# The tail of a four-layer kernel without six groups of filler matrix products on TensorE

## The reference, cut to what matters

```python
# third layer, feed-forward: a router picks 8 of 64 experts, and each expert is only a bias row
logits = flat @ router_weight.T + router_bias
scores = softmax(logits)
topk_w, topk_idx = top_k(scores, 8)
w_dense = zeros((T, E)).at[arange(T)[:, None], topk_idx].add(topk_w)
out = flat * topk_w.sum(-1, keepdims=True) + w_dense @ expert_bias

# fourth layer, attention: channels split by the top 60% of the context's channels, then gated
mask = one-hot of top_k(channel_map, k)
crucial, sub = mask * x, (1 - mask) * x
A1 = sigmoid(relu(norm(conv1d([max(crucial), mean(crucial)], conv_w))))
A2 = sigmoid(relu(norm(conv1d([max(sub), mean(sub)], conv_w))))
out = crucial * A1 + sub * A2

# fourth layer, feed-forward: a dense product and 2 of 8 low-rank adapters
out = x @ Wb.T + bias + 2 * sum over 2 of 8 adapters e of p_e * (x @ A_e.T) @ B_e.T
```

## Time and profile before

| what | value |
|---|---|
| median of 3 runs | 857.73 us (855.31 to 858.05) |
| the profiled execution | 857.56 us |
| its span | 855.9 us |
| TensorE busy | 774.1 us, 90% |
| VectorE busy | 709.6 us, 83% |
| ScalarE busy | 517.4 us, 60% |
| mean granted TensorE clock, share of full speed | 0.976 |
| start of the tail's work | 777.42 us |

### The profile page before, as it was taken

One profiled execution on the slowest core, in us unless ns is written; L12 is line 12 of the kernel. 1 busy time (PEld: TensorE's weight loads), 2 busy tenths in 40 slices (PEclk: granted clock), 3 DMA queues, 4 the chain that ended last, 5 costly groups with the idle time before them and its releaser, 6 DMA issues. The chain is left out here.

```text
span 855.9 us, 16356 instructions
## 1 busy us (share of the span) xinstructions
PE 774.1 (90%) x5134; PEld 629.4 (74%) x5140; DVE 709.6 (83%) x1752; ACT 517.4 (60%) x1407; POOL 432.1 (50%) x388
## 2 busy tenths in 40 slices
PE   1976799858988999999999999999999999888788
PEld 0474676534677898898898888888888889765347
DVE  7878998969787887887897897897898898786876
ACT  6865798746466657557557657657656565531521
POOL 3237078715036745844845845746646655573110
PEclk9999999979999999999999999999999999999989
DMA  8254236544120310310320320320320210003001
GB/s 313 92 167 155 76 131 223 175 133 144 30 71 22 115 39 9 99 65 0 98 74 0 98 74 0 98 74 0 98 74 0 74 59 15 25 1 120 1 0 50
DMA packets 37773, 66.15 MB, mean 77 GB/s; under 512 B 5537, under 2 KB 17889, under 8 KB 37602
## 3 DMA queue, kind: packets, MB, share of 16 engines
q1 hardware_dynamic: 37730, 65.63, 23.5%
HBM read 60.28 MB, written 5.34 MB: 77 GB/s over the span
## 5 line engine op out<-in xcount | busy, mean ns | idle before, releaser
L2042 ACT ACTIVATE layer_attention_probs<-xnT,stats 128x512 f32<-128x512 f32 x128 | 93.9, 734 | 132.6 <-DVE stats L2177 132.6
L2395 DVE TENSOR_SCALAR_CACHE_REDUCE xn<-ctxT,candidate 128x512 bf16<-128x512 f32 x240 | 168.8, 741 | 0.0
L1781 PE MATMUL bank<-layer_attention_keysT,layer_attention_queriesT 128*128 128x512 f32 x384 | 121.3, 424 | 5.0 <-DVE layer_attention_queriesT L2170 5.0
L2189 DVE TENSOR_TENSOR layer_attention_probsT<-bank,layer_attention_probsT 128x512 fp32r<-128x512 f32 x128 | 88.2, 689 | 41.7 <-ACT layer_attention_probsT L2050 40.3
L1781 PEld LDWEIGHTS bank<-layer_attention_probsT,layer_attention_values 128*128 128x128 f32 x768 | 99.1, 190 | 17.4 <-DVE layer_attention_probsT L2189 6.7
L1781 PE MATMUL bank<-layer_attention_probsT,layer_attention_values 128*128 128x256 f32 x768 | 102.6, 283 | 8.1 <-DVE layer_attention_probsT L2189 6.6
L2050 ACT CAST layer_attention_probsT<-bank 128x512 fp32r<-128x512 f32 x128 | 74.8, 585 | 48.0 <-PE bank L1858 47.9
L1781 PE MATMUL bank<-layer_attention_l_wq,layer_attention_xnT 128*128 128x512 f32 x408 | 99.3, 392 | 0.0
L1781 PEld LDWEIGHTS bank<-layer_attention_l_wkv,layer_context_parts 128*128 128x128 f32 x720 | 88.4, 188 | 2.7
L1781 PE MATMUL bank<-layer_attention_l_wkv,layer_context_parts 128*128 128x256 f32 x720 | 90.4, 278 | 0.0
L1781 PE MATMUL bank<-layer_attention_wo,layer_attention_headsT 128*128 128x512 f32 x336 | 88.8, 406 | 0.0
(11 more groups left out here) (337 smaller groups left out, 1664.7 us busy)
## 6 DMA issues: line engine op xcount, KB each, us to landing
layer_attention_l_raw_qo<-in_wqT SPq DMA_DIRECT2D x8, 1024.0 KB, 5.5
layer_attention_l_raw_qo<-in_woT SPq DMA_DIRECT2D x8, 1024.0 KB, 6.4
xnT<-inverse_sums SPq DMA_DIRECT2D x15, 512.0 KB, 3.7
tw_raw<-in_w_gateT SPq DMA_DIRECT2D x8, 688.0 KB, 5.4
tw_raw<-in_w_upT SPq DMA_DIRECT2D x8, 688.0 KB, 4.3
tw_raw<-in_w_downT SPq DMA_DIRECT2D x6, 768.0 KB, 4.7
layer_attention_l_raw_kv<-in_wkvT SPq DMA_DIRECT2D x8, 512.0 KB, 4.9
ternary<-tw_rounded SPq DMA_DIRECT2D x8, 344.0 KB, 2.6
```

Of the source, the lines that this page charges most:

```text
L1781: last = pe.matmul(out, stationary[f][a], moving[f][b], start=f == 0 and x == 0, stop=f == count - 1 and x == 2)
L2042: a.activation(probs[:, u % 3, :], masked[:, u % 2, :], ACT.Exp, bias=negmax[:, u:u + 1], scale=-1.0, accum_out=sums[:, u:u + 1]).then_inc ...
L2189: v.tensor_tensor(probsT[:, 1, p % 2, :, columns], T[u % 2][:, :].rearrange("p (c q) -> p c q", c=CPB), probsT[:, 0, p % 2, :, columns], A ...
L2395: own(k.nc.vector.tensor_scalar((k.flags if flags is None else flags)[:, r % 2], row_tile(k.ctxT, r), k.candidate[:, r:r + 1].bitcast(F32) ...
```

## The change

The six calls of `keep_busy` and the helper itself are taken out. All other instructions on all engines are the same and in the same order; only line numbers behind the helper are lower by 5 to 11.

```diff
--- before.py
+++ after.py
@@ -2549,11 +2549,6 @@
 
             @block.tensor
             def _(pe):
-                def keep_busy(bank, count):
-                    for _ in range(count):
-                        pe.matmul(k.bank[bank][:, :], k.ident16[:, :],
-                                  k.ident16[:, :].unsqueeze(1).broadcast_to([P, KT, P]), start=True, stop=True)
-
                 def turn(n, t):
                     pe.wait_ge(k.tile_xn, TILES * (n0 + n) + t + 1)
                     if t >= 2 and n < 2:
@@ -2572,13 +2567,11 @@
                     if t == TILES - 1:
                         last.then_inc(S_["logits_psum"], 1)
 
-                keep_busy(7, 16)
                 turn(0, 0)
                 for t in range(1, TILES):
                     turn(0, t)
                     expert_logits(t - 1)
                 expert_logits(TILES - 1)
-                keep_busy(7, 18)
                 pe.wait_ge(S_["dense_ready"], 1)
                 for t in range(TILES):
                     last = pe.transpose(k.bank[3][0:EXPERTS, t * P:(t + 1) * P], dense[:, t, :], k.ident[:, :])
@@ -2588,11 +2581,9 @@
                     pe.matmul(k.bank[4 + t][:, :], denseT[:, t * P:(t + 1) * P], ebias[:, :],
                               start=True, stop=True).then_inc(S_["mix_psum"], 1)
 
-                keep_busy(3, 10)
                 for t in range(TILES):
                     turn(1, t)
                 pe.wait_ge(S_["x_mixed"], TILES)
-                keep_busy(7, 24)
                 pe.wait_ge(S_["band_loaded"], 48)
                 pe.wait_ge(S_["features_ready"], 1)
                 for j, (blk, c) in enumerate((blk, c) for blk in (1, 0, 2) for c in range(2)):
@@ -2605,7 +2596,6 @@
                     pe.wait_ge(S_[ready], 1)
                     pe.matmul(k.bank[bank][:, 0:16], k.ones[:, :], source[:, :, :, :].rearrange("p f r b -> p (f r b)"),
                               start=True, stop=True).then_inc(S_[done], 1)
-                keep_busy(7, 20)
                 for t in range(TILES):
                     pe.wait_ge(S_["gated_ready"], KT * (t // TPB + 1))
                     for f in range(KT):
@@ -2626,7 +2616,6 @@
                             pe.matmul(last_bank(t)[:, :], xnT2[:, a, f, t * P:(t + 1) * P], wb[:, b, f, :],
                                       start=f == 0 and i == 0, stop=False, skip_group_check=True)
 
-                keep_busy(3, 22)
                 pe.wait_ge(S_["x_gated"], TILES)
                 for t in range(TILES):
                     turn(2, t)
```

## The result

| | before | after |
|---|---|---|
| median of 5 runs each | 858.05 us (855.31 to 861.33) | 866.04 us (863.80 to 868.89) |
| profiled execution, its span | 857.56, 855.9 us | 864.13, 862.4 us |
| mean granted clock, profiled execution | 0.976 | 0.950 |

The ratio is 1.0084, interval 1.0053 to 1.0115: slower by 7.2 us, 4.5 to 9.9. The text goes by this ratio; the two medians themselves lie 8.0 apart. Forecast were 863.2 us, 5.5 above the median shown before the change, and slower; the measured ratio puts that median of 857.73 at 864.9, inside the forecast's own range of 861.3 to 865.6.

The account below looks back on a forecast made before the run. TensorE, busy 774.1 of 855.9 us, was taken as the bound nearly everywhere, with a chain of waits in the tail. Terms 3.0 + 0.5 + 0 + 1.5 - 0.6 + 1.2 = +5.6 on 857.56 gave 863.2 us, range 861.3 to 865.6.

Parts of the forecast that it names:

- the overruns: Filler outlasting its wait before the first turn and before the back-transposes; removal priced at -2.1 and -0.6 us.
- A: Tail's start to router logits: first turn and router products at low clock throughout, +3.0 us.
- B: Experts' mix, router logits to second turn: transposes and four products slower at low clock, +0.5 us, bounds 0 and 0.7.
- Rival 1: Clock comes back during the router section, which then costs -0.1 us; sum +2.5, 860.1 us; chance 25%.
- the first step: Whole kernel: TensorE, busy 774.1 of 855.9 us, sets the end nearly everywhere.
- 2.1 us of overrun goes: First turn: its transposes waited behind 16 filler products though xn was ready at 780.6; start gains 2.1 us.
- C: Second turn: its 16 transposes ran at 0.50 already, so no change, 0; bounds -1.1 and 0 us.
- D: Convolution and sums: 12 records and the z product slower at low clock, +1.5 us, bounds +0.2 and +1.7.
- E: Gate and back-transposes: without overrunning filler the first transposed tile is ready earlier, -0.6 us.
- F: Last turn and final products: turn starts at low clock, which returns later, +1.2 us, bounds 0.5 and 2.0.
- Rival 2: Last turn and final products: clock does not come back behind transposes, 3.1 us in place of 1.2; 865.1 us; chance 8%.

Follow-up runs that it names:

- e1: Kernel before without the 16 filler products in front of the first turn, other five groups kept; timed ratio 1.0052 (1.0031 to 1.0073).
- e4: Kernel before with filler cut from 16 to 7 products ahead of the first turn and 20 to 12 ahead of the back-transposes; ratio 1.0038 (1.0013 to 1.0064).
- e5: Kernel before without the 18 filler products ahead of the wait for dense weights and the 10 ahead of the second turn; one run, 864.32 us.

## Why the prediction was right, point by point

- **Direction and mechanism.** Right: without filler TensorE's clock is low in the sections that the forecast named, and they take longer by more than the overruns gave back. In the two first profiles the tail grew by 5.6 us, and 5.6 was the sum. That they meet to the decimal is luck: A was 0.4 too high and B 0.5 too low, and before's first profile had an A that most others lack. Rival 1 (clock back during A) did not come in either profile of after. What the first step said, that TensorE's 90% sets the end nearly everywhere, was wrong for this change: TensorE is 14.4 us less busy in after and the kernel is slower, since part of its busy time was filler.
- **A (+3.0, measured +2.6).** The clock did stay at 0.50 to the end of the router, and the first transpose came at 3.3. The narrow records went at 0.20 to 0.21 us (eight from 783.58 to 785.28, eight from 786.14 to 787.74), not 0.224. But the base was not typical: A is 9.5 in most profiles with the 16 products, and against that the loss is 4.3; against the mean of all eight (10.2) it is 3.7. The step that was mis-sized is "2.1 us of overrun goes": it was 1.8 in before's first profile and 0.2 in its second.
- **B (+0.5, bounds 0 and 0.7; measured +1.0).** Wrong in size and outside its bounds. I let the four products end at 801.0 by 1.7 us each and left out the last one's way out of the array (0.4 of their 7.19), which I had subtracted from the 3.70; and no product found the clock back. Together they take 7.19 us, the transposes 1.06.
- **C (0), D (+1.5), E (-0.6).** Measured +0.1, +1.4 and -0.7. In E VectorE was next late, as said. But the base varies here too, which one profile could not show. D is 8.85 in all four profiles without the 24 products. With them it was 7.4 four times and 7.8 once where all groups ahead were as in before, and 7.8 to 8.8 in the five profiles where an earlier group was missing or cut. So D's loss is not that of its own group alone. E with the 20 products in place was 3.8 to 4.0 four times and 3.2 three times.
- **F (+1.2, measured +1.1).** The turn to the first dense product took 0.86 more on the chain (forecast 0.95), and the clock came back at 841.5, 4.7 us behind the turn's start. Rival 2 (transposes do not bring it back) would have given 3.1. The clock did come back at 810.8, when TensorE had done nothing but the second turn's transposes since 807.1, behind 2.15 us of idle. The Trainium skill, "TensorE: Matmul & The Clock Gate", section "Part 4: PE-mode transpose", says that the full clock does not engage in transpose mode; for these transposes the trace disagrees.
- **What the sum did not hold.** Timed, the loss is 7.2 us (4.5 to 9.9). Against the mean tail of before's two profiles (77.7) after's two (84.0) are 6.4 longer, which the interval holds. The 0.8 between them is not clear of noise. The profiled execution of after took 864.13 us, 0.9 over the forecast, since its tail also began 1.0 later. The part ahead of the tail, whose instructions are the same, ended between 777.4 and 784.3 us in 14 profiles. The two of before and the two of after lie among the seven earliest, those of e1 and e4 between 781.8 and 784.3, and e1 and e4 were timed slower than their tails say. Whether that part depends on what the tail holds, or 14 profiles were just few, stays open.

## What to carry to other kernels

Filler on an engine whose clock falls in waits has two prices and one return: it delays what is behind it if it outlasts the wait; at low clock it takes about twice as long (ten of these products took 4.45 us at 0.50 in e4's first profile, and 2.33 in before); and it makes it likelier, not certain, that the sections that follow run at the high clock. Count both per wait, and ask first which sections are long and depend on the clock: here the two groups ahead of the router section and the mix carried most of the loss, and the four others together 1.8 us in the profile, which the timing could not tell from nothing. Profile the same kernel more than once before a figure from one execution becomes the base of a sum.

## What the runs showed that was not expected

- The same 16 products took 5.30 us in one execution of the same kernel and 3.61 in another, and A was 11.2 and 9.5. The stretches took few values: A 9.5, 11.2, 12.4 or 13.8 for most, E 3.2 or 3.8 to 4.0. So the loss from taking filler out has no single value: it depends on what the kernel with filler did in that execution.
- The router section is the same in after and in e1, 16 transposes and 32 records of products, and started at low clock in both; the clock came back within its last 16 records in e1 and not at all in after, each in both profiles. It had fallen 0.3 us behind the tail's start in e1 and 1.7 behind it in after. And in after the four products of the mix took 7.2 us without a gap at 0.50, and the clock came back only behind the 16 transposes that follow. What decides that stays open.
- Idle TensorE does not lose the clock at a fixed point: in e5 the clock fell within its idle time ahead of the mix, in after it was low before that; and in after it stood at 1.00 for 3.2 us (810.9 to 814.1) in which TensorE did next to nothing.
